# Second attention of a hybrid block: value products of two head groups in one place, one transpose for the negated maxes

## The chip, the cores and the metric
One core of a Trainium2 chip runs the whole program. The metric is the device time of one execution in microseconds, the median of several runs. The engines are TensorE (PE; its weight loads are shown apart as PEld), VectorE (DVE), ScalarE (ACT), GpSimd (POOL) and SyncE (SP, which issues DMAs). They run side by side, each in its own order, and wait for each other by semaphores.

## The reference
`x` is 16 sequences of 256 tokens with 128 features. All is float32.

```python
x = x + attn_a(layernorm(x))        # one head of 128
x = x + ffn(layernorm(x))           # top-2 of 8 experts, capacity, plus a shared expert
x = x + attn_b(layernorm(x))        # 16 heads of 8, causal
x = x + ffn(layernorm(x))

# attn_b
qkv = encodings @ attn_W + attn_b                       # [b, n, 3 * 128]
q, k, v = split(qkv.reshape(b, n, 16, 24).transpose(0, 2, 1, 3), 3, axis=-1)
scores = einsum('bhki,bhqi->bhkq', k, q) / sqrt(8)
scores = where(k_index <= q_index, scores, -10000.0)
prob = softmax(scores, over k)
out = einsum('bhkq,bhkl->bhql', prob, v).transpose(0, 2, 1, 3).reshape(b, n, 128)
return out @ out_W + out_b
```

## The kernel before
Four stages follow each other: the first attention, the first MoE, the second attention, the second MoE. The change lies in the second attention (`attn_b_pair` on each engine).

**Tiling.** A sequence has 16 heads of 8 features, handled in four groups of four heads (`GRP` = 4, index g). Sequences come in pairs: i is the pair, h or `par` the one of the two, n = 2i + h. U = 4n + g counts the groups, 64 in all. PSUM has eight banks of 512 float32 per partition: AB (two) for the first pass, CB (two) for the second, OB for the value products, MB for the turned maxes, XB and ZB for projections and the way back.

**The work of one group** on TensorE goes through four steps, and the loop is software-pipelined so that one turn of it handles four groups at different steps:
- `pass1` (L878 to L883), three parts k = 0, 1, 2: scores with the queries on the partitions, plus the causal mask as a second matmul. DVE takes the negated maxes of each part into `negp` (L1752).
- `neg_transpose` (L892), one turn later: two transposes turn `negp`, one for each half of the queries (columns 96 to 127 of each half hold the maxes). ACT copies rows 96 to 127 of the result into `qc` (`neg_copy`, L1225), as the extra rows that subtract the max.
- `pass2` (L903 for k = 0, 1; L907 for k = 2), two turns later: scores with the keys on the partitions, minus the max. ACT takes exp into `pt` (L1232), POOL then zeroes the masked places with two selects (`causal`, L583), which both wait for the last of the three exps.
- `values` (L926), three turns later: eight matmuls (16 records in the trace), head j writes rows 32j to 32j+31 of OB. Only 9 of the 32 columns of `v_ext` are filled: 8 features and a column of ones for the sum. A group takes half of OB's 512 columns; after every second group ACT copies OB to `oT` (`o_copy`, L1201).

Behind `pass2` k = 2 each turn has one extra block by g: g = 0 `on_transpose` (L966) and `b_transpose` (L936); g = 1 `b_project` (L945, L949); g = 2 `out_project` (L974) and parts of the router (L705, L712, counts); g = 3 `o_back` (L959), eight transposes of `oT` into XB and ZB. DVE's `divide` (L1778, L1782) then divides by the sums.

**The order by hand.** Each engine's list is its program order. On TensorE a turn is: pass1 k=0, neg_transpose, pass1 k=1, pass2 k=0 and 1, pass1 k=2, values, pass2 k=2, the extra block. ACT: o_copy if due, small copies, neg_copy, three exps, then norms (L1245 in h=1, g=2; L1257 in h=0, g=1), `place_v` (L1238) in g=3. POOL: the rstd of a norm if due (L487 or L513), causal, adding the output bias (L590), one dispatch of router rows (L530, an indirect DMA). DVE: the three maxes with router steps between, `combine` (L1739) in g=0, `split` in g=2. SP: `restack` brings q and k of a later sequence through DRAM into `bdk` and `qc` (L397, L400).

**Waits that matter here.** `values` waits for `aff_done` (both selects of its group) and in the first group of a sequence for `ot_ready` (OB copied). `pass1` k waits until the maxes two parts back are taken, `pass2` k until the exp two parts back has read its bank, both as each pair of banks alternates. The second MoE starts behind the last groups; its rows come from POOL's dispatches.

## Time and profile before

| what | value |
|---|---|
| runs | 831.84, 834.34, 833.57 us; median 833.57 |
| profiled execution | 834.5 us |
| its span, first to last instruction | 832.8 us |
| mean granted TensorE clock | 0.971 |
| busy: PE / PEld / DVE / ACT / POOL | 758.8 / 688.7 / 493.7 / 440.6 / 431.7 us |
| second attention, loop of groups | about 329 to 612 us of the span |

The times of the rows below are from the profiled execution, in us from the start of the span. A matmul's duration overlaps those of the next ones; what a block costs is the distance between its start and the start of what follows.

### The profile page before, as it was taken

The page shows a single profiled execution, that of the slowest core. Times are in us where ns is not written, and L with a number is a line of the kernel's source. Part 1 is how long each engine was busy: PE and PEld are TensorE (multiplying, and loading weights), DVE is VectorE, ACT ScalarE, POOL GpSimd, SP SyncE. Part 2 cuts the span into 40 slices and gives each one's busy share as a digit, 9 for nine tenths or more (in the row PEclk, how much of TensorE's full clock was granted, in tenths as well). Part 3 has the DMA queues.
Part 4 walks back from the last instruction along what each step waited for, and adds up shares of the span by engine and source line. Part 5 has one row for each costly group of instructions (what it writes and reads, how often), then busy time and mean ns, then how long its engine had stood idle before and what let it go on. Part 6 is the DMA issues. An engine that isn't in the chain of part 4 may idle for free. (4 is left out here: it accounts for less than half of the span.)

```text
span 832.8 us, 18726 instructions
## 1 busy us (share of the span) xinstructions
PE 758.8 (91%) x6472; PEld 688.7 (83%) x6472; DVE 493.7 (59%) x1626; ACT 440.6 (53%) x1071; POOL 431.7 (52%) x545
## 2 busy tenths in 40 slices
PE   5877789699999997999999999999989599999994
PEld 4777789599999995777877787877779599999994
DVE  4777864245444455767777777867666244444437
ACT  2545455144444443676767766776655144444456
POOL 3347777155555551334344665665576255555530
PEclk9999979799999999999999999999999799999999
DMA  7981111233333224233223342223111233334138
GB/s 258 317 346 53 48 42 55 67 101 99 96 116 102 71 89 124 84 106 114 77 78 94 109 128 91 81 84 98 37 39 41 68 87 101 96 98 127 53 91 233
DMA packets 78164, 87.42 MB, mean 105 GB/s; under 512 B 12744, under 2 KB 66602, under 8 KB 77944
## 3 DMA queue, kind: packets, MB, share of 16 engines
q1 hardware_dynamic: 67872, 68.60, 26.7%
q0 software_dynamic: 9216, 17.34, 6.1%
q8 instruction: 53, 0.87, 0.4%
q10 hardware_dynamic: 984, 0.29, 0.2%
q14 instruction: 39, 0.32, 0.1%
HBM read 48.59 MB, written 39.65 MB: 106 GB/s over the span
## 5 line engine op out<-in xcount | busy, mean ns | idle before, releaser
L1172 ACT ACTIVATE hT<-bank,bias_T 128x256 f32<-128x256 f32 x448 | 175.5, 475 | 216.4 <-PE bank L815 216.3
L545 POOL DMA_INDIRECT y_rows<-yo,row_cur x160 | 157.7, 985 | 147.1 <-DVE yo L1662 119.0
L1752 DVE TENSOR_REDUCE negp<-bank 128x2 f32<-128x512 f32 (+1 forms) x192 | 128.3, 687 | 70.4 <-PE bank L879 67.4
L836 PE MATMUL bank<-w_s,hT 128*128 128x128 f32 x1280 | 156.0, 275 | 0.0
L530 POOL DMA_INDIRECT x_slots<-xr,slot_u x128 | 129.4, 1011 | 41.3 <-issue 33.9
L836 PEld LDWEIGHTS bank<-w_s,hT 128*128 128x128 f32 x1280 | 150.1, 192 | 0.0
L583 POOL TENSOR_SCALAR_AFFINE_SELECT pt<-pt 128x512 f32<-128x512 f32 x128 | 79.4, 642 | 124.2 <-ACT pt L1232 124.0
L1232 ACT ACTIVATE pt<-bank 128x512 f32<-128x512 f32 x192 | 107.7, 596 | 60.4 <-PE bank L907 50.6
L815 PE MATMUL bank<-xT_hl,w_hl 128*128 128x256 f32 x960 | 136.3, 292 | 3.5 <-DVE w_hl L1635 2.7
L815 PEld LDWEIGHTS bank<-xT_hl,w_hl 128*128 128x128 f32 x960 | 121.6, 193 | 4.2 <-DVE w_hl L1635 3.1
L1662 DVE TENSOR_TENSOR yo<-bank,b_b 128x256 f32<-128x256 f32 x80 | 34.0, 425 | 146.4 <-PE bank L836 146.4
L836 PE MATMUL bank<-sw_s,hT 128*128 128x128 f32 x512 | 64.7, 281 | 0.9 <-issue 0.5
L882 PE MATMUL bank<-bdk,qc 96*128 96x512 f32 x128 | 61.1, 477 | 3.4 <-DVE negp L1752 3.3
L836 PEld LDWEIGHTS bank<-sw_s,hT 128*128 128x128 f32 x512 | 62.0, 198 | 1.3 <-issue 1.3
L926 PE MATMUL bank<-pt,v_ext 128*32 128x256 f32 (+1 forms) x1024 | 54.9, 332 | 3.6 <-POOL pt L583 2.8
L815 PE MATMUL bank<-xT_hl,sw_hl 128*128 128x256 f32 x384 | 54.8, 293 | 2.9 <-issue 2.4
L815 PEld LDWEIGHTS bank<-xT_hl,sw_hl 128*128 128x128 f32 x384 | 48.9, 194 | 4.0 <-issue 3.2
L926 PEld LDWEIGHTS bank<-pt,v_ext 128*32 128x32 f32 x1024 | 26.9, 109 | 30.5 <-issue 12.4
L907 PEld LDWEIGHTS bank<-qc,bdk 128*128 128x128 f32 x256 | 33.4, 190 | 14.4 <-ACT pt L1232 11.0
L1552 DVE CAST xT_hl<-bank 128x256 fp32r<-128x256 f32 x80 | 33.2, 415 | 19.1 <-PE bank L786 19.1
L786 PE MATMUL bank<-ident,xg 128*128 128x128 f32 x160 | 31.3, 281 | 14.0 <-DMA xg<-x_slots 14.0
L907 PE MATMUL bank<-qc,bdk 128*128 128x128 f32 x256 | 42.5, 288 | 1.3 <-ACT pt L1232 1.1
(205 smaller groups left out, 1263.0 us busy)
## 6 DMA issues: line engine op xcount, KB each, us to landing
xg<-x_slots SPq DMA_DIRECT2D x80, 136.0 KB, 2.1
w_s<-in_L_ffn_w SPq DMA_DIRECT2D x32, 256.0 KB, 3.2
qk_rows<-qks SPq DMA_DIRECT2D x16, 512.0 KB, 4.0
bdk<-qk_rows SPq DMA_DIRECT2D x192, 32.0 KB
qc<-qk_rows SPq DMA_DIRECT2D x48, 128.0 KB, 2.9
x_slots<-xg SPq DMA_DIRECT2D x1, 5440.0 KB, 21.2
y_rows<-xg SPq DMA_DIRECT2D x1, 4096.0 KB, 16.2
bdk<-y_rows SPq DMA_DIRECT2D x1, 4096.0 KB
```

What stands on the lines that cost most here:

```text
L530: pool.indirect_dma_start(x_slots, bass.IndirectOffsetOnAxis(ap=slot_u[:, c, t:t + 1], axis=0), xr[:, t, :], None, bounds_check=E * CAP - ...
L545: pool.indirect_dma_start(y_rows, bass.IndirectOffsetOnAxis(ap=row_cur[:, g % ROWS, j:j + 1], axis=0), yo[:, g % RING, j, :], None, bounds ...
L583: a = pool.affine_select(out=blk, in_=blk, compare_op=ALU.is_ge, fill=0.0, base=0, pattern=[[0, 4], [1, P]], channel_multiplier=-1)
L815: m = pe.matmul(bk[:, (f % 2) * 256:(f % 2) * 256 + 256], wt[:, wp, f * P:(f + 1) * P], xT_hl[:, w % 2, xp, :], start=(p == 0), stop=(p == 2))
L836: m = pe.matmul(yb(w, l)[:, j * P:(j + 1) * P], hT[:, w % 2, f, j * P:(j + 1) * P], wt[:, f, :], start=(f == 0), stop=(f == FT - 1))
L882: pe.matmul(bk[:, :], q, bdk[0:96, par, g, 2 * k - 2:2 * k, :], start=True, stop=False)
L907: m = pe.matmul(bk[:, j * P:j * P + P], bdk[:, par, g, j, P:SEQ], qc[:, par, g, P:SEQ], start=True, stop=True)
L926: m = pe.matmul(OB[32 * j:32 * j + 32, c0 + kt * P:c0 + SEQ], v_ext[:, par, kt, 4 * g + j, :], rhs, start=(kt == 0), stop=(kt == 1))
L1172: a = act.activation(hT[:, w % 2, f, :], HB[2 * (w % 2) + f // 2][:, (f % 2) * 256:(f % 2) * 256 + 256], ACT.Silu, bias=bias_T[:, b0 + f:b ...
L1232: act.activation(pt[:, g % 2, k, :], CB[(g + k) % 2][:, :], ACT.Exp).then_inc(S.exp_done, 1)
L1662: dve.tensor_tensor(yo[:, g % RING, :, :], rows, b2_b[:, e:e + 1, :].broadcast_to([P, CH, D]), ALU.add).then_inc(S.yo_ready, 1)
L1752: dve.tensor_reduce(dst, AB[(g + k) % 2][:, :].rearrange("p (j k) -> p j k", j=heads), AX.X, ALU.max, negate=True).then_inc(S.amax_done, 1)
```

## The change
The value matrix of a head gets its nine columns at 0 to 8 of its 32 in groups 0 and 2, at 16 to 24 in groups 1 and 3, and zeros elsewhere. Two groups can then be summed in the same place of OB: group 1 adds into the rows and columns of group 0. OB holds a whole sequence, is copied once, and `oT` takes up two blocks of 256 columns; `o_back` makes four transposes into XB alone, and `divide` is one reciprocal and one product. The rows of `out_W` are loaded in the new order of heads, by eight DMAs. The maxes of the first half of the queries stay at columns 96 to 127 of `negp`, those of the second go to columns 64 to 95 of the same tile, so one transpose turns both; `neg_copy` becomes two copies, of rows 96 to 127 and 64 to 95. `place_v` becomes two instructions. On TensorE `values` moves ahead of `pass1` k = 2. At the loop's end ACT's first o_copy of the last sequence falls away.

```diff
+WB_LOADS = 11
...
-        negp = sb("negp", [P, 2, 2, P])
+        negp = sb("negp", [P, 2, P])
...
-            sp.dma_start(ow[:, :], out_W).then_inc(S.wb_in, 16)
+            for gg in range(2):
+                for j in range(4):
+                    sp.dma_start(ow[64 * gg + 16 * j:64 * gg + 16 * j + 16, :],
+                                 out_W.rearrange("(a b j d) n -> a j b d n", a=2, b=2, j=4)[gg, j]).then_inc(S.wb_in, 16)
...
             def neg_transpose(t, par, g):
...
-                for qt in range(2):
-                    m = pe.transpose(MB[:, qt * P:qt * P + P], negp[:, g % 2, qt, :], ident[:, :])
-                m.then_inc(S.negT_done, 1)
+                pe.transpose(MB[:, 0:P], negp[:, g % 2, :], ident[:, :]).then_inc(S.negT_done, 1)
...
             def values(t, par, g):
...
-                if g % 2 == 0:
-                    need(pe, S.ot_ready, 2 * n + g // 2)
-                c0 = (g % 2) * SEQ
+                if g == 0:
+                    need(pe, S.ot_ready, n)
+                c0 = (g // 2) * SEQ
...
-                                      start=(kt == 0), stop=(kt == 1))
+                                      start=(kt == 0 and g % 2 == 0), stop=(kt == 1 and g % 2 == 1))
...
             def o_back(t, par):
...
                 for qt in range(2):
-                    for g in range(GRP):
-                        m = pe.transpose((XB, ZB)[qt][:, g * P:(g + 1) * P], oT[:, g, qt * P:(qt + 1) * P], ident[:, :])
+                    for gg in range(2):
+                        c = SEQ * qt + P * gg
+                        m = pe.transpose(XB[:, c:c + P], oT[:, gg, qt * P:(qt + 1) * P], ident[:, :])
...
                             pass2(*g2, 1)
+                        if valid(g3[0]):
+                            values(*g3)
                         if valid(i):
                             pass1(i, h, g, 2)
-                        if valid(g3[0]):
-                            values(*g3)
...
-            def o_copy(t, par, half):
+            def o_copy(t, par):
                 n = 2 * t + par
-                act.wait_ge(S.pv_done, GRP * n + 2 * half + 2)
+                act.wait_ge(S.pv_done, GRP * (n + 1))
...
             def neg_copy(t, par, g):
...
-                act.activation(qc[96:P, par, g, :], MB[96:P, 0:SEQ], ACT.Copy).then_inc(S.neg_set, 1)
+                act.activation(qc[96:P, par, g, 0:P], MB[96:P, 0:P], ACT.Copy)
+                act.activation(qc[96:P, par, g, P:SEQ], MB[64:96, 0:P], ACT.Copy).then_inc(S.neg_set, 1)
...
-                        if g % 2 == 1 and valid(t):
-                            o_copy(t, par, g // 2)
+                        if g == 3 and valid(t):
+                            o_copy(t, par)
```

## Rows read from the trace of the kernel before

**Rows 1.** The page, busy time of an engine, its share, instructions
```profile
PE 758.8 (91%) x6472; PEld 688.7 (83%) x6472; DVE 493.7 (59%) x1626; ACT 440.6 (53%) x1071; POOL 431.7 (52%) x545
```
**Rows 2.** Waits of PE, 325:620: who for whom, us, times, longest
```profile
PE bank L926 <- POOL pt L583: 2.8, 3, 1.3
```
**Rows 3.** Timeline, PE, behind transposes: start us, us, engine, line, instruction, out and in
```profile
449.64 0.67 PE L907 MATMUL bank<-qc,bdk 128*128 128x128 f32 x4
...
451.07 0.38 PE L892 MATMUL bank<-ident,negp 128*128 128x128 f32 x2
451.21 0.48 PE L882 MATMUL bank<-bdk,qc 96*128 96x512 f32 x1
...
451.65 0.64 PE L903 MATMUL bank<-qc,bdk 128*128 128x256 f32 x4
452.13 0.46 PE L882 MATMUL bank<-bdk,qc 96*128 96x512 f32 x1
...
452.64 0.86 PE L926 MATMUL bank<-pt,v_ext 128*32 128x256 f32 x16
453.42 0.66 PE L907 MATMUL bank<-qc,bdk 128*128 128x128 f32 x4
```
**Rows 4.** Timeline, PE, a round with o_back
```profile
445.43 0.67 PE L907 MATMUL bank<-qc,bdk 128*128 128x128 f32 x4
445.93 1.06 PE L959 MATMUL bank<-ident,oT 128*128 128x128 f32 x8
446.74 0.47 PE L878 MATMUL bank<-bdk,qc 96*128 96x512 f32 x1
```
**Rows 5.** Timeline, PE and POOL, the loop's first round with values
```profile
339.41 0.66 PE L907 MATMUL bank<-qc,bdk 128*128 128x128 f32 x4 [1.13 <-ACT pt L1232]
...
340.77 1.24 POOL L583 TENSOR_SCALAR_AFFINE_SELECT pt<-pt 128x512 f32<-128x512 f32 x2 [12.66 <-ACT pt L1232]
...
342.07 0.86 PE L926 MATMUL bank<-pt,v_ext 128*32 128x256 f32 x16
342.85 0.66 PE L907 MATMUL bank<-qc,bdk 128*128 128x128 f32 x4
```
**Rows 6.** Timeline, DVE and POOL, combine beside the selects
```profile
450.16 1.13 DVE L1739 SCALAR_TENSOR_TENSOR x<-yab,gate,x 128x128 f32<-128x128 f32 x4
...
451.01 1.37 POOL L583 TENSOR_SCALAR_AFFINE_SELECT pt<-pt 128x512 f32<-128x512 f32 x2 [2.99 <-ACT pt L1232]
```
**Rows 7.** Timeline, ACT, the round with norms
```profile
458.80 0.60 ACT L1232 ACTIVATE pt<-bank 128x512 f32<-128x512 f32 x1 [0.90 <-PE bank L907]
...
461.23 0.57 ACT L1201 ACTIVATE oT<-bank 128x512 f32<-128x512 f32 x1
461.83 0.38 ACT L1225 ACTIVATE qc<-bank 32x256 fp32r<-32x256 f32 x1
462.23 1.08 ACT L1232 ACTIVATE pt<-bank 128x512 f32<-128x512 f32 x2
```
**Rows 8.** Timeline, L907 and the exps ahead of it in two more rounds
```profile
458.10 0.67 PE L907 MATMUL bank<-qc,bdk 128*128 128x128 f32 x4
...
462.88 0.67 PE L907 MATMUL bank<-qc,bdk 128*128 128x128 f32 x4
...
475.95 1.09 ACT L1232 ACTIVATE pt<-bank 128x512 f32<-128x512 f32 x2
...
476.66 0.55 PE L907 MATMUL bank<-qc,bdk 128*128 128x128 f32 x3
```
**Rows 9.** Timeline, PE, third pass1 behind DVE
```profile
506.49 0.50 PE L882 MATMUL bank<-bdk,qc 96*128 96x512 f32 x1 [0.90 <-DVE negp L1752]
```
**Rows 10.** Timeline, SP's loads of bdk and the first pass1 that needs them
```profile
418.14 4.87 SPq L397 DMA_DIRECT2D bdk<-qk_rows  x12
...
428.42 0.19 PEld L878 LDWEIGHTS bank<-bdk,qc 96*128 96x128 f32 x1 [0.30 <-DMA qc<-qk_rows]
```
**Rows 11.** Timeline, POOL, behind the loop
```profile
626.17 0.20 POOL L511 TENSOR_SCALAR ve<-mv 128x4 f32<-128x4 f32 x1
```

More of the change, by code:

```diff
@@ L571, in attn_b_consts @@
                 pool.tensor_copy(ident_r[:, :], ident[:, :])
-                pool.memset(negp[:, :, :, :], 0.0)
+                pool.memset(negp[:, :, :], 0.0)
                 pool.memset(v_ext[:, :, :, :, 0:HD], 0.0)
-                pool.memset(v_ext[:, :, :, :, HD + 1:32], 0.0)
-                pool.memset(v_ext[:, :, :, :, HD:HD + 1], 1.0).then_inc(S.init_b, 1)
+                pool.memset(v_ext[:, :, :, :, HD + 1:16 + HD], 0.0)
+                pool.memset(v_ext[:, :, :, :, 16 + HD + 1:32], 0.0)
+                by_group = v_ext[:, :, :, :, :].rearrange("p a k (c b j) r -> p (a k c) b (j r)", c=2, b=2)
+                for b in range(2):
+                    for at in range(2):
+                        col = by_group[:, :, b, :].rearrange("p c (j r) -> p c j r", r=32)[:, :, :, 16 * at + HD:16 * at + HD + 1]
+                        a = pool.memset(col, 1.0 if at == b else 0.0)
+                a.then_inc(S.init_b, 1)
             def causal(t, par, g):
@@ L1237, in place_v @@
                 need(act, S.pv_done, GRP * (n - 1))
-                act.activation(v_ext[:, par, :, :, 0:HD], v_s[:, par, :, :].rearrange("p k (h d) -> p k h d", d=HD), ACT.Copy
-                               ).then_inc(S.v_set, 1)
+                for b in range(2):
+                    a = act.activation(v_ext[:, par, :, :, :].rearrange("p k (c b j) r -> p (k c) b j r", c=2, b=2)[:, :, b, :, 16 * b:16 * b + HD],
+                                       v_s[:, par, :, :].rearrange("p k (c b j d) -> p (k c) b j d", c=2, b=2, d=HD)[:, :, b], ACT.Copy)
+                a.then_inc(S.v_set, 1)
             def norms_b(q):
@@ L1303, in attn_b_end @@
                 silus(1, 0)
-                o_copy(t, 1, 1)
+                o_copy(t, 1)
                 silus(1, 1)
@@ L1750, in max_b @@
                 heads, first = (4, 0) if k == 0 else (2, 2 * k - 2)
-                dst = negp[:, g % 2, min(k, 1), 96:P].rearrange("p (j r) -> p j r", r=8)[:, first:first + heads, 0]
+                c0 = 64 if k else 96
+                dst = negp[:, g % 2, c0:c0 + 32].rearrange("p (j r) -> p j r", r=8)[:, first:first + heads, 0]
                 dve.tensor_reduce(dst, AB[(g + k) % 2][:, :].rearrange("p (j k) -> p j k", j=heads), AX.X, ALU.max,
@@ L1775, in divide @@
                 need(dve, S.onT_done, n)
[L1776 to L1779 removed]
+                o = XB[:, :].rearrange("p (q r) -> p q r", r=16)
+                dve.reciprocal(osum[:, :, :].rearrange("p q h -> p (q h)"), o[:, :, HD]).then_inc(S.osum_ready, 1)
                 dve.wait_ge(S.osum_ready, n + 1)
[L1781 to L1784 removed]
+                dve.tensor_tensor(on[:, :, :, :].rearrange("p q h d -> p (q h) d"), o[:, :, 0:HD],
+                                  osum[:, :, :].rearrange("p q h -> p (q h)").unsqueeze(2).broadcast_to([P, 2 * HEADS, HD]),
+                                  ALU.mult).then_inc(S.on_ready, 1)
             def add_out(t, par):
@@ L1894, in _ @@
             moe(0, 0, ITEMS - 1)
-            dve.wait_ge(S.wb_in, 16 * 4)
+            dve.wait_ge(S.wb_in, 16 * WB_LOADS)
             dve.wait_ge(S.init_b, 1)
```

17 lines of the change are left out of this document (4 added, 13 removed).

## The prediction
> **What bounds the kernel now.** I read the page's busy times first: TensorE is busy 91% of the span [rows 1], no other engine much over half of it. The change lies in the second attention, from 339 us (the first L907 of the loop) to 610 us, so next I read the waits of that stretch [rows 2]: TensorE's own idle time there comes to a few us (2.8 us in front of the values, behind the causal selects of POOL). TensorE runs back to back. The timeline of its instructions then gives the price of each part, as the distance between starts, since the durations overlap.
>
> I call the stretch from the first matmul of one L907 block to that of the next a round: four extra blocks take turns behind L907 (g=0: the transposes L966 and L936, g=1: the projections, g=2: out projection and router, g=3: o_back), then come pass1 k=0, the neg transposes, pass1 k=1, pass2 k=0 and 1, pass1 k=2, the values (L926), and L907 again. One round behind g=0 reads [rows 3]: L907 at 449.64, the third pass1 (L882) at 452.13, values at 452.64, next L907 at 453.42, 3.78 us in all.
>
> **What is taken away.** Two neg transposes stand at 451.07 and the matmul behind them at 451.21, so the pair takes 0.14 us; eight transposes of o_back take 445.93 to 446.74, 0.81 us or 0.10 each [rows 3, 4]. The matmul that follows starts close behind the last transpose, so what falls away with one of two is a whole distance between starts and not half of 0.14: 0.11 us, one such distance, as 0.81 less the short last one over seven gives. One neg transpose fewer is 0.11 us a round (64 rounds, 7.0 us) and four fewer in o_back are 0.44 us a sequence (16, 7.0 us). If TensorE alone set the pace this would be 14.0 us.
>
> **What the moved line does.** The values now stand in front of pass1 k=2. The move changes no work, but it changes what must be ready. The values wait for the causal selects of their group, and these hang on the L907 of the round before: L907, exp, two selects. Early in the loop, where there is no extra block, this chain is seen bare [rows 5]: L907 at 339.41, selects 340.77 to 342.01, values at 342.07. So values can't start earlier than 2.66 us behind L907. From the values to the next L907 it is 0.78 us now. With pass1 k=2 in between it is 0.44 us more (the same pair of matmuls L882 and L883 takes 451.21 to 451.65 [rows 3]; the 0.51 before the values holds the change of array shape, which then comes behind L903 instead). The chain alone now asks for 2.66 + 0.78 + 0.44 = 3.88 us a round, where it asked for 3.44. TensorE's own work in the round of rows 3 is 3.78 - 0.11 = 3.67. The cover that hid POOL is gone: values would start at 452.13 - 0.11 + 0.09 = 452.11, 2.47 behind L907, and must wait.
>
> **Round by round**, old length against the new bound (lengths between L907 starts in the timeline; the classes hold 14, 15, 15 and 16 rounds up to the loop's end, and one more that is named):
> - Behind o_back (14 rounds): 449.64 - 445.43, old 4.21 [rows 3, 4]; TensorE 3.67, chain 3.88. -0.34 each, but one of them (at 428.42) already waits for the DMA of qc [rows 10] and gains nothing: 13 x -0.34 = -4.4 us.
> - Behind the transposes (15): old 3.78, chain 3.88. In seven of them DVE's combine (L1739) runs beside the selects, and the pair takes 1.37 us instead of 1.24 [rows 5, 6]; the new place lies 0.3 us deeper in the combine, so I take +0.28 each, +2.0. Three rounds lack one of the two pairs of transposes, two times 0.11 less cover: +0.3 each, +0.9. Three stall today because the third pass1 waits for a max on DVE (L882 at 506.49, 0.90 us [rows 9]); the values now fill that hole: -0.8 each, -2.4. Two more at +0.1. Sum +0.7.
> - Behind the projections (15): there is cover (458.10 - 453.42 = 4.68 us [rows 3, 8]), so -0.11 in eight. In four, ACT is the bound: the two exps start at 475.95, the first ends 0.60 later [rows 7], just ahead of L907 at 476.66 [rows 8], and neg_copy stands in front of it, see below; +0.1 each. Two near the loop's end have no projections and so no cover (+0.4 each), and in one POOL comes late behind a dispatch (+0.3): +1.1. Sum +0.6.
> - Behind out projection and router (16): oT must be copied before the first values of the next sequence overwrite the bank. ACT does that behind four norms, at 461.23 to 461.80 [rows 7]; the next L907 starts at 462.88 [rows 8], 4.78 us behind the one at 458.10. With values pulled forward the copy still ends at 3.70 behind L907, and pass1 k=2 comes on top: 3.70 + 0.15 + 0.78 + 0.44 = 5.07, +0.3 in five rounds (0.15 from the copy to the values is an estimate, between the 0.06 behind the selects of rows 5 and the 0.21 to the values here). The first round (old 342.85 - 339.41 = 3.44, no extra block) [rows 5] and its follower cost 3.88 - 3.44 = +0.44 each, +0.9; the other ten gain 0.07 each. Sum +1.7.
> In all -4.4 + 0.7 + 0.6 + 1.7 = **-1.4 us**.
>
> **The other edits.** neg_copy becomes two ACT instructions of half the columns. The trace has one of 32x256: 0.38 us, the next begins 0.40 behind it [rows 7]. Two of 32x128 cost between +0.02 (only columns count) and +0.40 (twice the same); I take +0.15, nearer to the lower end, as an exp of 512 columns lasts 0.22 more than this copy of 256 [rows 7], so 128 columns fewer are 0.11 less: 2 x 0.27 = 0.54 against 0.40 if nothing overlaps. It is used above in the four ACT rounds; elsewhere the first exp ends well before L907 and hides it. The oT copy (0.57 us [rows 7]) goes from two to one a sequence, out of the round where ACT is fullest (+0 to -0.2 us, taken at zero). place_v in two pieces costs 0.03 to 0.41 us a sequence in ACT time behind the exps of g=3, where ACT then waits: hidden. One reciprocal and one product instead of two each shorten divide; only the three DVE rounds could feel it. Accumulating over two groups changes flags, not the count of matmuls: 0, at worst a few ns each. On SP seven more loads of ow stand early in the queue (twelve loads of bdk take SP 4.87 us [rows 10], so some 0.4 each, 2.8 us), ahead of the expert weights of the first MoE, which are used only after the whole first attention: hidden, and 2.8 us at most if not. POOL's extra memsets lie ahead of a long wait of POOL's for DVE: hidden. Behind the loop POOL runs a train of dispatches right behind the last causal selects and only then, at 626.17, rstd2 [rows 11], which the last routing hangs on; so the shift of the last causal selects carries through to the end one to one, and the four transposes saved in the last o_back are lost behind that train.
>
> The profiled execution took 834.5 us, so it would come to 833.1; the runs' median is 833.57, 0.9 lower, and I predict 833.57 - 1.4 = **832.2 us**.
>
> **The rivals.**
> (1) TensorE count: values wait for nothing, all 14.0 us come, 819.6 us. For it: TensorE is back to back today. Against: the bare chain of rows 5. Chance 0.06.
> (2) The chain binds, but the small costs don't: halved neg copies nearly free (-0.8), the DMA round gains after all (-0.7), selects no longer than today beside the combine (-0.7). -3.6, 830.0 us. Chance 0.22.
> (3) Slower: the selects stretch. They now lie on the path in 28 rounds, and they share something with DVE: beside the combine the pair took 0.13 more [rows 5, 6]. If DVE work catches them in all 28 at 0.2 us, 28 x 0.2 = 5.6, and it ends at -1.4 + 5.6 = +4.2, 837.8 us. It decides from 0.05 us a round for a loss at all, 0.14 for one that can be measured. The maxes (L1752) are most of DVE's work and showed no such effect in rows 5. Chance 0.12. "SBUF — State Buffer" of the Trainium skill (SBUF: two separate sides) states this as a rule: DVE with two SBUF inputs and GpSimd lock each other out for a whole instruction. The trace agrees as far as rows 6 go.
> (4) The change doesn't do what it says, the place in the order being held by something else: no change, 833.6. Chance 0.02.
> Forecast: 0.58.
>
> **Chances.** A measurement of this kernel can tell about 0.3%, 2.5 us. Faster by more: (1), most of (2) and a tail of the forecast, 0.30. Slower by more: most of (3), 0.10. Within: 0.60. The range holds the forecast with its bounds (neg copies 0 to +1.0 us, selects 0 to +2.5, more rounds held by DMA +1) and (2), and leaves out (1) and the far end of (3): 828.8 to 836.2.
>
> **What would show it.** In the trace of the changed kernel: L926 directly behind L903, with waits for POOL of about 0.2 us in about half the rounds; rounds behind o_back and behind the transposes equally long, near 3.9 us; the rounds with norms longer by 0.3 us. TensorE's busy time falls by more than the span does. It is wrong if values start less than 2.6 us behind L907, or if the selects pair takes over 1.5 us.

## The result and the profile after

The changed kernel takes 828.59 us (median of 7 runs, 826.76 to 831.59) beside 833.37 us for the kernel before on the same chip (7 runs): a ratio of 0.9945, interval 0.9922 to 0.9968. That is 4.8 us less, where 1.4 us less was predicted; it lies 0.2 us below the low end of the range. Taken again later (`changed_again`, below) the ratio was 0.9956 [0.9939, 0.9974].

The page of the changed kernel, span and busy times (engine, us, share, instructions), to set against rows 1:
```profile
span 825.0 us, 18482 instructions
PE 747.4 (91%) x6344; PEld 677.0 (82%) x6344; DVE 501.4 (61%) x1594; ACT 444.7 (54%) x1135; POOL 436.0 (53%) x549
```
TensorE lost 11.4 us of busy time and the kernel 4.8: more than half of the saving went elsewhere. The timeline of TensorE says where to look. The first line is the loop's first L919 block (L907 before), the second its last:
```profile
336.84 0.66 PE L919 MATMUL bank<-qc,bdk 128*128 128x128 f32 x4 [1.19 <-ACT pt L1246]
602.20 0.66 PE L919 MATMUL bank<-qc,bdk 128*128 128x128 f32 x4
```
and the same last block in the kernel before:
```profile
609.59 0.66 PE L907 MATMUL bank<-qc,bdk 128*128 128x128 f32 x4
```
So the loop of 63 rounds went from 609.59 - 339.41 [rows 5] = 270.2 us to 602.20 - 336.84 = 265.4 us, -4.8 us. What follows it stayed (832.8 - 609.6 = 223.2, 825.0 - 602.2 = 222.8). That this trace enters the loop 2.6 us earlier comes from the earlier stages, which vary by themselves: the second trace of the same kernel enters it at 339.7, has the same 265.4 and a span of 827.8, and the second trace of the kernel before enters it at 338.0 instead of 339.4. In what follows I compare loops, cut into rounds as in the prediction.

The waits of the stretch 325 to 610 (engine, tile and line, for whom; us, times, longest), to set against rows 2:
```profile
PEld bank L938 <- POOL pt L597: 18.0, 34, 1.5
PE bank L938 <- POOL pt L597: 7.2, 16, 1.3
```
Before, the values (now L938) waited 2.8 us for POOL in three places, now 7.2 us in 16 (and their weight load, which runs ahead, waits in 34 rounds, before in 17): the move made a new wait, as forecast. Two rounds in the timeline, behind o_back and behind the transposes (TensorE's rows, and those of POOL and DVE that bear on them), to set against rows 3, 4 and 6:
```profile
441.69 0.56 PE L919 MATMUL bank<-qc,bdk 128*128 128x128 f32 x4
442.08 0.63 PE L972 MATMUL bank<-ident,oT 128*128 128x128 f32 x4
442.47 0.48 PE L892 MATMUL bank<-bdk,qc 96*128 96x512 f32 x1
442.95 1.22 POOL L597 TENSOR_SCALAR_AFFINE_SELECT pt<-pt 128x512 f32<-128x512 f32 x2 [2.96 <-ACT pt L1246]
...
444.23 0.86 PE L938 MATMUL bank<-pt,v_ext 128*32 128x256 f32 x16
445.01 0.50 PE L896 MATMUL bank<-bdk,qc 96*128 96x512 f32 x1
...
445.48 0.56 PE L919 MATMUL bank<-qc,bdk 128*128 128x128 f32 x4
...
446.29 1.88 DVE L1754 SCALAR_TENSOR_TENSOR x<-yab,gate,x 128x128 f32<-128x128 f32 x4
...
446.74 1.28 POOL L597 TENSOR_SCALAR_AFFINE_SELECT pt<-pt 128x512 f32<-128x512 f32 x2 [2.57 <-ACT pt L1246]
...
449.33 0.56 PE L919 MATMUL bank<-qc,bdk 128*128 128x128 f32 x4
```
Four transposes of o_back take 0.39 us (442.08 to 442.47) where eight took 0.81. The selects end at 444.17 and the values start at 444.23: POOL's chain sets this round, 3.79 us long (4.21 before). Behind the values the next L919 comes 1.25 us later. Note L919 itself: 0.56 us for its four matmuls, where L907 took 0.67 [rows 3, 4], and 0.39 to what follows where it was 0.50 (over six such rounds of each trace 0.40 and 0.50). This is the first thing the prediction had not seen. The second round, with the combine beside the selects, takes 3.85 us.

The 63 rounds by what lies in them, kernel before against changed kernel (lengths between block starts, us):

| rounds | predicted | measured | of it |
|---|---|---|---|
| behind o_back, 14 | -4.4 | -5.8 | nine at -0.44 each, four in which DVE is late at -0.30; the one held by the DMA of qc [rows 10] -0.6, the DMA wait did not recur |
| behind the transposes, 16 | +0.7 | +1.0 | seven with combine +0.07 each, +0.5; three where DVE is late 4.87 to 4.67, -0.6; the rest +1.1 |
| behind the projections, 15 | +0.6 | -1.1 | eight at -0.18 each; five bound by ACT 4.68 to 4.70; the two near the loop's end -0.07 and +0.35 |
| behind out projection and router, and the first rounds, 18 | +1.7 | +1.1 | first round and follower +0.8; with norms +0.07 in three and +0.21 in two; one with out projection alone +0.5; the other ten -0.09 each |
| sum | -1.4 | -4.8 | |

### The profile page after: what moved, and what is told of

Same layout as the page of the kernel before. It is cut to its first block and busy times, and to the rows that moved or that the text cites. A ratio compares the mean times of both kernels' runs of the same rounds, so it can differ in the third digit from the quotient of the medians.

```text
span 825.0 us, 18482 instructions
## 1 busy us (share of the span) xinstructions
PE 747.4 (91%) x6344; PEld 677.0 (82%) x6344; DVE 501.4 (61%) x1594; ACT 444.7 (54%) x1135; POOL 436.0 (53%) x549
## 5 line engine op out<-in xcount | busy, mean ns | idle before, releaser
L1768 DVE TENSOR_REDUCE negp<-bank 128x2 f32<-128x512 f32 (+1 forms) x192 | 130.4, 687 | 63.5 <-PE bank L897 32.7
L597 POOL TENSOR_SCALAR_AFFINE_SELECT pt<-pt 128x512 f32<-128x512 f32 x128 | 84.3, 680 | 116.6 <-ACT pt L1246 116.2
L850 PE MATMUL bank<-sw_s,hT 128*128 128x128 f32 x512 | 66.8, 287 | 0.9 <-issue 0.5
L896 PE MATMUL bank<-bdk,qc 96*128 96x512 f32 x128 | 63.1, 493 | 2.9 <-DVE negp L1768 2.6
L938 PE MATMUL bank<-pt,v_ext 128*32 128x256 f32 (+1 forms) x1024 | 54.9, 332 | 11.8 <-POOL pt L597 7.2
L850 PEld LDWEIGHTS bank<-sw_s,hT 128*128 128x128 f32 x512 | 64.1, 203 | 1.3 <-issue 1.3
L938 PEld LDWEIGHTS bank<-pt,v_ext 128*32 128x32 f32 x1024 | 27.2, 109 | 33.5 <-POOL pt L597 18.0
L896 PEld LDWEIGHTS bank<-bdk,qc 96*128 96x128 f32 x128 | 25.0, 195 | 21.1 <-issue 8.3
L915 PE MATMUL bank<-qc,bdk 128*128 128x256 f32 x256 | 41.0, 282 | 0.0
```

What stands on the lines that cost most here:

```text
L597: a = pool.affine_select(out=blk, in_=blk, compare_op=ALU.is_ge, fill=0.0, base=0, pattern=[[0, 4], [1, P]], channel_multiplier=-1)
L850: m = pe.matmul(yb(w, l)[:, j * P:(j + 1) * P], hT[:, w % 2, f, j * P:(j + 1) * P], wt[:, f, :], start=(f == 0), stop=(f == FT - 1))
L896: pe.matmul(bk[:, :], q, bdk[0:96, par, g, 2 * k - 2:2 * k, :], start=True, stop=False)
L915: m = pe.matmul(bk[:, j * SEQ:j * SEQ + SEQ], bdk[:, par, g, 2 * k + j, 0:P], qc[:, par, g, :], start=True, stop=True)
L938: m = pe.matmul(OB[32 * j:32 * j + 32, c0 + kt * P:c0 + SEQ], v_ext[:, par, kt, 4 * g + j, :], rhs, start=(kt == 0 and g % 2 == 0), stop=( ...
L1768: dve.tensor_reduce(dst, AB[(g + k) % 2][:, :].rearrange("p (j k) -> p j k", j=heads), AX.X, ALU.max, negate=True).then_inc(S.amax_done, 1)
```

## The experiments

`same`, `move_only`, `unmoved` and `ow_only` shared a chip with each other (before 832.32 us); `early_sel`, `mix`, `max_half` and `pack_only` another one, on which everything outside the loop is slower (before 881.05 us), so of those only ratios and loops are used (the granted clock in their loops is 0.99 to 1.00, in the others 1.00); `changed_again`, `pack_move`, `some_early` and `some_early_two` shared a third (before 832.95 us). All diffs are against the changed kernel unless said.

**same**: the kernel before once more.

> The kernel before once more, for its trace. In the changed kernel's trace 2.6 us of the 7.8 us less span lie ahead of the second attention's loop of groups. Theory E (early stages vary by themselves): the two stages ahead of the loop take another time here than in the first trace of the kernel before (first L907 at 339.4 us), by 1 us or more either way, while the loop (first to last L907, 270.2 us) is the same within 0.3 us. Theory S (the change's loads or memsets shortened the early stages): first L907 at 339.4 within 0.5 us again.

Measured: 833.12 us, ratio 1.0011 [0.9995, 1.0028]; loop 269.8, as the DMA wait of rows 10 was absent (that round 4.22 instead of 4.55). So 0.3 us of the kernel before was that wait, and 269.8 is the loop to compare with. It enters the loop at 338.0, so the earlier stages do vary by themselves.

**ow_only**: kernel before with `ow` loaded in eight pieces.
```diff
-            sp.dma_start(ow[:, :], out_W).then_inc(S.wb_in, 16)
+            for k in range(8):
+                sp.dma_start(ow[16 * k:16 * k + 16, :], out_W[16 * k:16 * k + 16, :]).then_inc(S.wb_in, 16)
```


> The kernel before with ow loaded by eight DMAs of 16 rows (the wait counts raised), nothing else. Theory E (early stages vary by themselves): total as before, 833.4 within 0.3%; the first L907 anywhere between 335 and 340 us. Theory S (the loads shift the early DMAs so that the early stages end sooner): total 2 to 4 us less, first L907 at 335 to 337 us.

Measured: 832.96, ratio 1.0004 [0.9989, 1.0018], loop 269.8, entered at 339.6. The seven more loads neither cost nor gain anything that can be told.

**move_only**: kernel before with the values moved ahead of the third pass1, nothing else.
```diff
+                        if valid(g3[0]):
+                            values(*g3)
                         if valid(i):
                             pass1(i, h, g, 2)
-                        if valid(g3[0]):
-                            values(*g3)
```


> Only the values are moved ahead of pass1 k=2; nothing else of the change. Theory A (what the changed kernel's trace suggests: the four L907 matmuls are dearer when they follow the values, so that behind pass1 the block is 0.1 us shorter, the chain from L907 to the values 2.54 us instead of 2.66, and TensorE's round 0.07 us shorter where it sets the pace): rounds behind o_back 4.15 us, rounds behind the transposes 3.8 to 3.9, three DVE holes filled (0.8 us each), loop 268 us, 2 us less than before. Theory B (the prediction's prices): chain 2.66, rounds behind o_back 4.21, behind the transposes 4.0, loop 271 us, 1 us more than before.

Measured: 832.47, ratio 1.0002 [0.9987, 1.0017], loop 270.6. The rounds with cover get shorter without any work removed (behind projections 4.68 to 4.61), those without cover longer (3.79 to 3.85 with combine, 3.45 to 3.90 and 3.43 to 3.78 in the first two). The shortening is L907's: directly behind the values its four matmuls take 0.50 us to what follows, behind pass1 0.40. Pass1 in that place loses 0.03 us (0.47 in the changed kernel from its start to the next L919, 445.01 to 445.48, as against 0.44 for the same pair elsewhere [rows 3]). The values use the array in another shape, and in the traces the first weight load behind them starts together with its matmul, where behind pass1 it runs 0.12 us ahead; that the shape is the cause is argued, no run takes it apart. The rounds came out as theory A has them, but not its loop of 268: the three rounds in which DVE is late got 0.2 us shorter and not 0.8, and those without cover got longer by more.

**unmoved**: the changed kernel with the values back behind the third pass1.
```diff
-                        if valid(g3[0]):
-                            values(*g3)
                         if valid(i):
                             pass1(i, h, g, 2)
+                        if valid(g3[0]):
+                            values(*g3)
```


> The changed kernel with the values back behind pass1 k=2: all transposes saved, the move undone. Theory A and B agree that the selects are covered again: rounds behind o_back 4.21 - 0.55 = 3.67 us, behind the transposes 3.67, behind the projections 4.57; the rounds with norms 4.78 as before, DVE holes of 1 us stay. Loop some 10 us shorter than before (260 us), total near 823 us, so the move costs 5 us of what the change could bring. Rival C (the loop has a further bound near what the changed kernel shows, for instance DVE or ACT): loop 264 to 266 us, total as the changed kernel's 828.6.

Measured: 828.45, ratio 0.9961 [0.9944, 0.9978], loop 265.6: as fast as the change. The rounds show a surprise. One neg transpose is gone from each, values wait for nothing new, and still the rounds behind the projections are 4.68 us and behind the transposes 3.78, as in the kernel before. A round of the kernel before (behind o_back, timeline of DVE, PE and its weight loads, PEld):
```profile
447.56 0.69 DVE L1752 TENSOR_REDUCE negp<-bank 128x4 f32<-128x512 f32 x1 [1.58 <-PE bank L879]
...
447.86 0.64 PE L903 MATMUL bank<-qc,bdk 128*128 128x256 f32 x4
...
448.31 0.18 PEld L882 LDWEIGHTS bank<-bdk,qc 96*128 96x128 f32 x1
448.34 0.47 PE L882 MATMUL bank<-bdk,qc 96*128 96x512 f32 x1
...
448.64 0.28 PE L883 MATMUL bank<-cmask,ident_r 128*128 128x256 f32 x1
```
and the same round of `unmoved`:
```profile
443.06 0.69 DVE L1768 TENSOR_REDUCE negp<-bank 128x4 f32<-128x512 f32 x1 [1.16 <-PE bank L905]
...
443.26 0.63 PE L915 MATMUL bank<-qc,bdk 128*128 128x256 f32 x4
...
443.81 0.19 PEld L896 LDWEIGHTS bank<-bdk,qc 96*128 96x128 f32 x1
443.81 0.50 PE L896 MATMUL bank<-bdk,qc 96*128 96x512 f32 x1
```
The third pass1 writes the bank that the max of the first part reads. That max ends at 443.75, and the weight load and the matmul of the third pass1 start 0.06 later. From L915 to the third pass1 it is 0.55 instead of 0.48, and from there to its mask matmul 0.34 instead of 0.30: 0.11, the whole transpose, is given back. And the kernel before was held by the same max already: there it ends at 448.25, and the weight load of the third pass1 starts 0.06 later too, at 448.31. Read from every round of the traces, that distance is 0.05 to 0.06 us in all 61 rounds with three parts of pass1, in the kernel before, in `same`, in `unmoved` and in `pack_only` alike. No wait is listed for it in most rounds because the weight loads in front of it have only just ended, and the matmul only follows its load.

**max_half**: `unmoved` with the max of the first part taken over half of its keys (that part of the computation is left out), so DVE's instruction is shorter.
```diff
-                dve.tensor_reduce(dst, AB[(g + k) % 2][:, :].rearrange("p (j k) -> p j k", j=heads), AX.X, ALU.max,
+                dve.tensor_reduce(dst, AB[(g + k) % 2][:, :].rearrange("p (j k) -> p j k", j=heads)[:, :, 0:64 if k == 0 else 256], AX.X, ALU.max,
```


> The kernel with the move undone, and the maxes of k=0 taken over 64 of the 128 keys (part of the maximum is left out, DVE's L1752 for k=0 gets some 0.27 us shorter). Theory D (in the old order the third pass1 waits for the max of k=0, 1.25 us behind the mask matmul of k=0, so that one neg transpose less saves nothing): rounds behind the transposes fall from 3.78 to 3.67, behind the projections from 4.68 to 4.57, behind o_back from 3.78 to 3.67; loop from 265.6 to 261 us or less. Rival F (the transpose's time is lost in TensorE itself, for instance to the weight load behind it): rounds stay at 3.78 and 4.68.

Measured: ratio 0.9851 [0.9815, 0.9886], loop 259.1, 6.5 us under `unmoved`. The timeline of the same round:
```profile
472.62 0.43 DVE L1768 TENSOR_REDUCE negp<-bank 128x4 f32<-128x256 f32 x1 [1.28 <-PE bank L905]
...
472.82 0.64 PE L915 MATMUL bank<-qc,bdk 128*128 128x256 f32 x4
...
473.18 0.19 PEld L896 LDWEIGHTS bank<-bdk,qc 96*128 96x128 f32 x1
473.29 0.40 PE L896 MATMUL bank<-bdk,qc 96*128 96x512 f32 x1
...
473.53 0.28 PE L897 MATMUL bank<-cmask,ident_r 128*128 128x256 f32 x1
```
The weight load now starts 0.13 us behind the max and 0.11 ahead of its matmul. L915 to the third pass1 is 0.47 again, from there to the mask matmul it is 0.24, and rounds behind o_back and behind the transposes fall to 3.60 us (3.78 in `unmoved`), further than to the 3.67 expected. The max of the first part was the bound of `unmoved`; shown. Of the 0.18 us, 0.11 is the transpose and 0.07 is what the max had cost the kernel before as well: TensorE's own count there was below the 3.78 that it took.

**pack_only**: only the values packed (with `ow`, one o_copy, four transposes in o_back), old order, two neg transposes and one neg copy.
```diff
-                pe.transpose(MB[:, 0:P], negp[:, g % 2, :], ident[:, :]).then_inc(S.negT_done, 1)
+                for qt in range(2):
+                    m = pe.transpose(MB[:, qt * P:qt * P + P], negp[:, g % 2, qt, :], ident[:, :])
+                m.then_inc(S.negT_done, 1)
...
-                act.activation(qc[96:P, par, g, 0:P], MB[96:P, 0:P], ACT.Copy)
-                act.activation(qc[96:P, par, g, P:SEQ], MB[64:96, 0:P], ACT.Copy).then_inc(S.neg_set, 1)
+                act.activation(qc[96:P, par, g, :], MB[96:P, 0:SEQ], ACT.Copy).then_inc(S.neg_set, 1)
```
(Not printed: `negp` and the places of the maxes as in the kernel before, and the values moved back as in `unmoved`.)

> The value products of two groups in one place, in the old order, with two neg transposes and one neg copy as before. Theory D (DVE's max bounds the old order): the rounds are those of the kernel with the move undone, 3.78 behind o_back and behind the transposes, and where ACT sets the pace they are shorter than there, for neg copy is not split: behind the projections 4.68 instead of 4.80 in four, in the rounds with norms 4.77 instead of 4.94 in five; loop 264 us, 1.3 less than with the single transpose. Rival: the single transpose is worth its 0.11 us a round after all, loop 270 or so less 6.5 for o_back, 263.5 plus, and 7 us more than with both parts is refuted already.

Measured: ratio 0.9934 [0.9910, 0.9957], loop 264.2. The rounds behind o_back lose 0.41 us each (thirteen, -5.3 us: twelve at 0.42 to 0.47, one, held by the max, at 0.10), every other kind is where it was in the kernel before, to 0.1 us in the sum of its rounds. One of the three parts alone does the whole of the change's work.

**pack_move**: the change with two neg transposes and one neg copy (the edits of `pack_only`, without moving the values back).

> The changed kernel with two neg transposes and one neg copy, so the neg edit alone is undone while the values stay ahead of the third first-pass matmul. Theory: in this order TensorE's own count bounds the rounds behind projections, so these get 0.10 to 0.18 us longer (4.50 to 4.60 or more), while the rounds behind o_back hang on POOL's selects and stay at 3.8; the nine rounds in which ACT is late give 0.1 back. Loop 265.5 to 267, time 0 to 1.5 us above the changed kernel. So the single neg transpose is worth about nothing in either order. Rival, the prediction's own count (0.11 us in each round that TensorE bounds, some 30 of them, and +0.15 for the split copy in four): loop 268 to 269.

Measured: 829.26, ratio 0.9952 [0.9937, 0.9968], loop 266.6. With it the four combinations are complete, all with packed values (loop, us; the kernel before had 269.8):

| | two neg transposes | one |
|---|---|---|
| values behind the third pass1 | 264.2 (`pack_only`) | 265.6 (`unmoved`) |
| values ahead of it | 266.6 (`pack_move`) | 265.4 (the change) |

In the old order the single transpose gains nothing and costs 1.4, all of it on ACT: two copies instead of one, +0.12 in five rounds behind the projections and +0.17 in five with norms. In the new order it gains 1.2. The move costs 2.4 with two transposes and gains 0.2 with one. Each alone is a loss on packed values, and both together still stand 1.2 us above `pack_only`; the ratios alone, with intervals of 0.3 to 0.5%, would not tell these four apart. The rounds do, though from one trace of each but the change: two traces of one kernel had loops that differ by under 0.1 us, the DMA wait aside.

**changed_again**: the changed kernel beside the three others of its chip.

> The changed kernel unaltered, beside the three others on the same chip. Its loop (first L907-type block to the last) took 265.4 us in its first trace, its time was 0.9945 of the kernel before. If most of the 4.8 us lies in the loop, the loop is 265.4 again within 0.5 and the ratio 0.993 to 0.997. If a part of it was luck in the early stages (the first trace entered the loop 2.6 us earlier), the loop still is 265.4 but the ratio comes nearer to 0.997.

Measured: 829.32, ratio 0.9956 [0.9939, 0.9974], loop 265.4, its rounds within 0.02 us of the first trace's. The gain is the loop's.

**mix**: the values ahead of the third pass1 only in rounds that had got shorter by it, behind it in the others.
```diff
-                        if valid(g3[0]):
+                        early = (g == 2 and 8 * i + 4 * h + g - 3 != 59) or (g == 3 and 8 * i + 4 * h + g - 3 not in (0, 8)) or (
+                            g == 1 and h == 0 and 3 <= i <= 5)
+                        if early and valid(g3[0]):
                             values(*g3)
                         if valid(i):
                             pass1(i, h, g, 2)
+                        if not early and valid(g3[0]):
+                            values(*g3)
```


> The changed kernel, with the values ahead of pass1 k=2 only in the rounds with cover (behind the projections, behind out projection and router but for the first two, and behind the transposes where combine and the router's steps fill DVE), and behind it elsewhere. From the rounds of the changed kernel and of the one with the move undone, each taken where it was the shorter: 0.1 to 0.5 us less in some 20 rounds, 3.9 us in all against the changed kernel, loop 261.5 us, total 824.7. If the rounds lean on each other (a round made shorter hands its wait to the next) the gain is under 2 us: loop 263.5 or more.

Measured: ratio 1.0011 [0.9985, 1.0037], loop 268.6: most of the gain gone. The timeline of one round behind o_back:
```profile
493.12 0.56 PE L919 MATMUL bank<-qc,bdk 128*128 128x128 f32 x4
...
494.03 0.86 DVE L1363 BATCH_NORM_STATS2 st<-x 128x6 f32<-128x128 f32 x4
...
495.88 0.65 DVE L1772 TENSOR_REDUCE negp<-bank 128x4 f32<-128x512 f32 x1
...
496.58 0.50 PE L896 MATMUL bank<-bdk,qc 96*128 96x512 f32 x1 [1.02 <-DVE negp L1772]
```
In the round before this one the values are early, so its last pass1 ends later and the last max is taken 0.20 us behind L919 (493.32); the norm's statistics (L1363) and router steps queue behind it on DVE, and the first max of this round behind them, ending at 496.53. In `unmoved` the same statistics start 0.11 behind L919 (458.67, with L919 at 458.56), 0.8 us earlier, and the round takes 3.77. On the way one of the router's steps (L1412 here, L1408 there), an instruction with two inputs beside the selects, takes 0.65 instead of 0.19. Here the third pass1 waits 1.02 us with nothing in the way to fill the gap, and the round takes 4.80 us; with the values early (the change, 458.67 to 462.59) they fill the hole and it takes 3.92. Rounds cannot be chosen one by one.

**early_sel**: the first causal select waits for the second exp alone.
```diff
-                pool.wait_ge(S.exp_done, 3 * U + 3)
-                for blk in (first, second):
+                for k, blk in enumerate((first, second)):
+                    pool.wait_ge(S.exp_done, 3 * U + 2 + k)
```


> The changed kernel, with the first causal select waiting for the second exp of its group instead of the third (it masks only what the first two wrote); the second select waits for the third as before. Nothing is left out. Theory P (POOL's chain of two selects behind the third exp sets the rounds without cover in the changed kernel): values no longer start 0.05 us behind the second select; rounds behind o_back fall from 3.79 to some 3.66 us, behind the transposes from 3.85 to 3.65, the loop from 265.4 to 261 us. Rival Q (the wait for POOL in these rounds hides another bound just behind it, DVE's maxes or ACT): rounds stay at 3.8, loop 264 to 265.

Measured: ratio 0.9921 [0.9893, 0.9949], loop 261.7. Behind o_back the rounds fall from 3.79 to 3.60 us, which is TensorE's own count: POOL's chain was the bound there. But of those with the combine, six rise to 4.46:
```profile
477.42 2.54 DVE L1754 SCALAR_TENSOR_TENSOR x<-yab,gate,x 128x128 f32<-128x128 f32 x4
...
477.87 0.65 POOL L597 TENSOR_SCALAR_AFFINE_SELECT pt<-pt 128x512 f32<-128x512 f32 x1 [0.79 <-ACT pt L1246]
...
478.49 1.32 POOL L604 TENSOR_TENSOR x<-x,ob_b 128x512 f32<-128x512 f32 x1
...
479.88 1.28 DVE L1768 TENSOR_REDUCE negp<-bank 128x4 f32<-128x512 f32 x2
...
480.62 0.50 PE L896 MATMUL bank<-bdk,qc 96*128 96x512 f32 x1 [0.79 <-DVE negp L1768]
```
The combine (four instructions) took 1.13 us before [rows 6], 1.88 in the change, and takes 2.54 where a select starts inside it and POOL's bias addition (L604) follows at once. The max waits behind it, and the third pass1 for the max. POOL's selects keep their 0.65 each. In two more rounds the trace has the select inside the combine and no bias addition behind it: the combine takes 1.51 and the round 3.61. It goes the other way as well: in the changed kernel a pair of selects that starts 0.01 us behind DVE's split (L1777) takes 1.77 us instead of 1.22, and the split keeps its 0.69 (rows of the rounds with norms, below). In these traces the instruction that starts second pays. This is the exclusion that the Trainium skill states in "SBUF — State Buffer", section "SBUF: two separate sides" (a DVE instruction with two SBUF inputs and a GpSimd instruction that reads SBUF shut each other out, and the one that starts first keeps the port for the whole instruction); the traces agree with it in these numbers.

**some_early**: `early_sel`, except in the two of eight groups whose round holds DVE's combine or its split.
```diff
-                pool.wait_ge(S.exp_done, 3 * U + 3)
-                for blk in (first, second):
+                for k, blk in enumerate((first, second)):
+                    pool.wait_ge(S.exp_done, 3 * U + (3 if U % 8 in (0, 2) else 2 + k))
```


> The changed kernel; POOL's first causal select of a group waits for the second exp alone and not for all three, except in the groups whose round holds DVE's combine or its split to fp32r (two of eight). With this for all groups the loop was 261.7 us, and the combine took 2.54 us instead of 1.13 beside the selects. Theory (the selects and DVE's two-input operations stretch one another): those two kinds of round go back to 3.85 and 4.6 us, the others keep 3.6 and 4.4 to 4.5; loop 256 us, 9 us under the changed kernel, ratio near 0.983. Rival (the long rounds came from POOL's own dispatch instructions or from the order of the exps, not from DVE): nothing gained over the version for all groups, loop 261 to 262.

Measured: 820.60 us, ratio 0.9857 [0.9834, 0.9881], loop 258.0: 8.7 us under the changed kernel on the same chip, and the fastest version that computes everything. The round behind o_back and the start of the next:
```profile
440.72 0.56 PE L919 MATMUL bank<-qc,bdk 128*128 128x128 f32 x4
...
441.98 0.64 POOL L597 TENSOR_SCALAR_AFFINE_SELECT pt<-pt 128x512 f32<-128x512 f32 x1 [0.78 <-ACT pt L1246]
...
443.08 0.86 PE L938 MATMUL bank<-pt,v_ext 128*32 128x256 f32 x16
...
444.33 0.56 PE L919 MATMUL bank<-qc,bdk 128*128 128x128 f32 x4
...
445.14 1.88 DVE L1754 SCALAR_TENSOR_TENSOR x<-yab,gate,x 128x128 f32<-128x128 f32 x4
```
Now one select and not two follows L919's exp; the values start 2.36 us behind L919 (2.54 in the change), 0.46 after the select has ended (442.62), so TensorE and no longer POOL sets this round, 3.61 us. The combine is back at the 1.88 us of the changed kernel and its rounds at 3.85; the rounds of the split fall from 5.12 to 4.59. The loop is 2 us longer than expected: against `early_sel` three rounds with norms go from 4.60 back to 4.84, and two early rounds with the split in them and little cover from 3.30 and 3.75 back to 3.91 and 4.33.

**some_early_two**: `some_early` with two neg transposes and one neg copy (the edits of `pack_only`, order as in the change).

> The kernel before this one in the list, with two neg transposes and one neg copy again. With POOL's selects early, TensorE's count bounds most rounds and the third first-pass matmul no longer waits for DVE, so here the single transpose should be worth its time on TensorE: 0.11 to 0.18 us in some 45 rounds, loop 5 to 8 us longer than with one transpose. Rival (the maxes on DVE bound these rounds): equal within 2 us.

Measured: 824.07, ratio 0.9889 [0.9871, 0.9908], loop 260.7. The single transpose is worth 2.7 us of loop here, where nothing else bounds the round: +0.12 in each round behind o_back (3.60 to 3.73) and in nine behind the projections, while with two transposes and one copy five of ACT's rounds there and four in which DVE is late get 0.09 shorter, and two with norms 0.20. That is half of the low end of the expectation, which counted 45 rounds at that price: six rounds with combine did not move, and ten of the fifteen behind out projection got no more than 0.05 us longer. How the packed values in the old order would do with POOL's selects early was not run, so what the move is worth there is open.

## Why the prediction was wrong, by its own steps

The step that failed is the price of the moved line. The prediction set TensorE's count (3.67 us for a round of rows 3) against POOL's chain (2.66 + 0.78 + 0.44 = 3.88) and took the larger. The count left out that the L907 block gets 0.10 us cheaper when it no longer follows the values, and the chain was measured from that same dearer L907: the runs show 2.54 us and not 2.66 from there to the values, rounds of 3.79 and not 3.88, and -0.18 and not -0.11 where there is cover. Both of the prediction's own signs of being wrong came: values less than 2.6 us behind L907, and a pair of selects over 1.5 us (1.77, in rounds with the split).

- **What bounds the kernel**: TensorE, back to back. Right for what the waits show, incomplete for what matters: in every round of the old order the weight load of the third pass1 hung on DVE's first max. The prediction saw this wait only in the three rounds where it was large [rows 9]. It follows that the 0.11 us a round for the neg transpose, 7.0 us, could not be had in the old order at all (`unmoved`, `pack_only`). What the move does is to put the values into that gap: in the changed kernel the third pass1 starts 0.85 us or more behind the max where TensorE sets the pace.
- **The chain of POOL** as new bound where there is no cover: right in kind. Values start 0.06 us behind the selects in the rounds that it bounds, and the waits for POOL came in about half the rounds, 34 by the list of waits. Wrong in size: 3.88 us was taken, 3.79 measured. The term that failed is the 2.66 us from L907 to the values, read from rows 5, where L907 still stood behind the values. In the new order it stands behind pass1, the exp comes 0.10 earlier, and the distance is 2.54. The prediction named the change of array shape and let it move to pass1, but did not take it out of the L907 from which it measured the chain. The other term, 0.78 + 0.44 = 1.22, is 1.25.
- **Rounds with cover**: -0.11 predicted, -0.18 measured, for the same reason: -0.11 for the transpose, -0.10 for L907, +0.03 for pass1. `move_only` shows the last two alone, 4.68 to 4.61.
- **The 3.4 us between -1.4 and -4.8**, summed over the rounds: -0.9 in nine rounds behind o_back and -0.6 in eight behind the projections, both from L907; -0.3 in four of ACT's rounds, where the earlier exp pays for the split copy; -0.6 for the DMA wait that did not recur; -0.8 in three rounds behind the projections that were set too high for lack of cover or for a dispatch; -1.5 in the rounds with combine and -0.9 in those with norms, both set too high. Against it stand +1.8 in the three rounds where DVE is late, +0.2 in four behind o_back that DVE holds, and +0.3 in what is left. That the sum missed by no more than this is in part luck: the errors at the combine and at DVE's late rounds, the largest two, nearly cancel.
- **Four transposes of o_back**: 0.44 counted, 0.42 measured (0.81 to 0.39), 0.42 to 0.47 kept in twelve of the thirteen rounds of `pack_only`.
- **Selects beside the combine**: +0.28 a round predicted, +0.07 measured. The pair took 1.28, not more than the 1.37 of rows 6; it is the combine that stretched, 1.13 to 1.88 us (in the three rounds where DVE is late it took 1.5 to 1.9 before), without anything waiting for it. Rival 3 had the kind of effect right. Beside the combine it is DVE's instructions that start second, and nothing waits for them until `early_sel`. Beside the split it is the selects, and in one round of the changed kernel, with out projection and no router behind L919, the values wait for them (timeline of that round):
```profile
370.85 1.77 POOL L597 TENSOR_SCALAR_AFFINE_SELECT pt<-pt 128x512 f32<-128x512 f32 x2 [3.28 <-ACT pt L1246]
...
372.68 0.86 PE L938 MATMUL bank<-pt,v_ext 128*32 128x256 f32 x16 [0.62 <-POOL pt L597]
```
  Its L919 stands at 369.59, so the values start 3.09 behind it, and the round takes 4.34 us instead of 3.81: +0.5 us that the sum had at -0.07.
- **Rounds where DVE is late**: -0.8 each predicted, -0.2 measured. The values do fill the hole, but DVE's queue moved back with them: the last max of the round before is taken later, what is behind it too, and in the first such round the third pass1 starts 4.21 us behind the round's L919, still waiting for the max, where it started 3.52 behind L907. `mix` shows the same coupling.
- **Rounds with norms**: +0.3 predicted, +0.07 measured in three. First the kernel before, then the changed kernel (timelines):
```profile
458.61 0.69 DVE L1761 TENSOR_TENSOR qks<-qk,qks 128x512 fp32r<-128x512 f32 x1
...
458.81 0.54 POOL L493 TENSOR_SCALAR nm<-mv 128x4 f32<-128x4 f32 x1
...
459.67 1.65 ACT L1245 ACTIVATE xn<-x,nb,rstd 128x128 f32<-128x128 f32 x4 [0.27 <-POOL nb L496]
```
```profile
453.83 0.56 PE L919 MATMUL bank<-qc,bdk 128*128 128x128 f32 x4
...
454.48 0.19 POOL L501 TENSOR_SCALAR nm<-mv 128x4 f32<-128x4 f32 x1
...
455.09 0.69 DVE L1777 TENSOR_TENSOR qks<-qk,qks 128x512 fp32r<-128x512 f32 x1
455.10 1.77 POOL L597 TENSOR_SCALAR_AFFINE_SELECT pt<-pt 128x512 f32<-128x512 f32 x2
455.15 1.65 ACT L1261 ACTIVATE xn<-x,nb,rstd 128x128 f32<-128x128 f32 x4
...
456.71 0.57 ACT L1214 ACTIVATE oT<-bank 128x512 f32<-128x512 f32 x1
...
457.31 0.27 ACT L1238 ACTIVATE qc<-bank 32x128 fp32r<-32x128 f32 x1
...
457.43 0.86 PE L938 MATMUL bank<-pt,v_ext 128*32 128x256 f32 x16 [0.23 <-ACT oT L1214]
457.59 0.27 ACT L1239 ACTIVATE qc<-bank 32x128 fp32r<-32x128 f32 x1
```
  The copy ends 3.45 us behind L919 and not 3.70, and the values start 0.15 behind it, as estimated; they wait 0.23 us for ACT. The 0.25 was in front of the norms: before, a small POOL instruction that they hang on (L493) ran beside DVE's split and took 0.54 us, now it is done ahead of the split in 0.19, and the norms start 1.32 us behind L919 instead of 1.57. The selects pay in its place (1.77 us), and for them nobody waits in these rounds, as the copy ends later.
- **The split neg copy**: two of 0.27 us, 0.28 apart: 0.54 as against 0.40, as estimated (+0.15). It shows in `unmoved` (+0.12 in ACT's rounds behind the projections, +0.17 in those with norms); in the change ACT's rounds behind the projections come out at +0.02, as the earlier exp pays for it.
- **Outside the loop**: the tail carries the loop's shift one to one (222.8 and 223.2 us), the loads of `ow` cost nothing (`ow_only`). Both right.
- **The chances**: a gain of over 0.3% had 0.30, and rival 2 (-3.6 us: the chain binds, the small costs don't come) was nearest to what happened, although of its three terms the copies came only in part, and L907 was not in it. That it came near is luck in the sum.

Still open: how the combine's stretch (0.38 us beside one select, 0.75 beside two, 1.41 beside a select and the bias addition) comes about in each of its four instructions was not taken apart, and neither was the DMA wait of rows 10, present in one of the two traces of the kernel before.

## What to carry to other kernels

This loop sat on two bounds at once, and the list of waits showed the second only in the few rounds where it was large. Before counting a saving on the busy engine, take for each block of the round the time at which its other inputs and its bank become ready, and set it against the start of the block's weight load and not only of its matmul. A distance that is the same in every round points to a wait. A chain measured in the old order holds for the new one only if the instructions in front of its start stay the same. Try the parts of a bundle alone and in pairs: here one of three parts made all of the gain, the other two lost a little each and together (though with the selects early the single transpose was worth 2.7 us of loop), and the next gain (8.7 us) lay in starting POOL's first select earlier in the rounds where DVE has no two-input work.

## What the runs showed of the hardware

- A block of four 128-column matmuls directly behind the 128x32-shaped value products takes 0.67 us, behind pass1's pair 0.56, and 0.50 instead of 0.40 to its successor; pass1's pair in the same place loses 0.03 (0.47 as against 0.44). "TensorEngine Tiling (Array Packing)" of the Trainium skill, section "Key Properties", says that a change of mode drains the array; the trace agrees that there is a price where the shape changes and adds that it depends on what comes behind; that the drain is its cause no run shows.
- Of a two-input DVE instruction and a GpSimd instruction that overlap, the one that started second gets longer: the combine's four from 1.13 to 1.88 and 2.54 us, the split's product from 0.69 to 1.08 (`early_sel`), a router step on 128x32 from 0.19 to 0.65, but two selects from 1.22 to 1.77 and a GpSimd instruction on 128x4 from 0.19 to 0.54 where DVE had started first.
- In the old order the weight load that precedes the overwriting of a PSUM bank starts 0.05 to 0.06 us behind the end of the DVE instruction that read the bank, in 61 rounds of 61; run freely it starts 0.11 to 0.12 ahead of its matmul (`max_half`), and a 512-column matmul whose load does not run ahead takes 0.34 to its successor instead of 0.23 to 0.24.
- A PSUM copy of 32x128 takes 0.27 us on ACT and one of 32x256 0.38 [rows 7]: halving the columns saves 0.11.
